# Weight-transpose evacuation in groups of four tiles, and the output store on SyncE's queue, in an eight-core recurrence-and-FFN layer

## The reference, cut to what matters

```python
# u: (4, 4096, 1024) f32; N = 256, HIDDEN = 3072
lam = sigmoid(einsum('btd,nd->btn', u, Wl) + bl)
Bu  = einsum('btd,nd->btn', u, Wb)
h_t = lam_t * h_(t-1) + Bu_t                      # scan over t, h_0 = 0
y   = einsum('btn,dn->btd', H, Wc) + u * Dp
x   = layernorm(u + y)                            # no scale, no bias, eps 1e-5
g   = einsum('bsd,hd->bsh', x, w_gate / 127)      # int32 weights
up  = einsum('bsd,hd->bsh', x, w_up / 127)
out = layernorm(x + einsum('bsh,dh->bsd', silu(g) * up, w_down / 127))
```

## Time and profile before

| | us |
|---|---|
| runs shown: lowest, highest, median of the two | 1896.27, 2077.3, 1986.78 |
| profiled execution, its own time | 1897.56 |
| span of its slowest core (core 7) | 1896.0 |
| spans of the eight cores | 1881.5 to 1896.0 |
| PE busy | 1450.9 (77%) |
| DVE busy | 394.2 (21%) |
| ACT busy | 414.2 (22%) |
| setup of the small weights, up to the first load of u | 0 to 54.3 |
| first matmul of the FFN (line 667) | 772.2 |
| end of the last matmul of the FFN (line 705), about | 1856.6 |

### The profile page before, as it was taken

One profiled execution on the slowest core, in us unless ns is written; L12 is line 12 of the kernel. 1 busy time (PEld: TensorE's weight loads), 2 busy tenths in 40 slices (PEclk: granted clock), 3 DMA queues, 4 the chain that ended last, 5 costly groups with the idle time before them and its releaser, 6 DMA issues.

```text
span 1896.0 us, 19628 instructions; the slowest of 8 cores (1881.5 to 1896.0 us)
## 1 busy us (share of the span) xinstructions
PE 1450.9 (77%) x7216; PEld 720.6 (38%) x7216; DVE 394.2 (21%) x628; ACT 414.2 (22%) x575; POOL 91.0 (5%) x177
## 2 busy tenths in 40 slices
PE   2493846738364333799997999997999997999993
PEld 1342433424222323344443444443444443444441
DVE  2330130401054232122102222103122103212103
ACT  2324142421323444211100311101211002111001
POOL 0001000010100000000010000010000011000010
PEclk9795876859598566899998999997999997999996
DMA  2517265280700000222221322221322222222121
GB/s 67 161 57 170 62 167 122 62 174 16 160 6 1 0 1 0 78 78 78 72 73 45 115 75 78 73 73 56 106 78 74 76 71 79 80 78 78 50 73 50
DMA packets 85165, 142.85 MB, mean 75 GB/s; under 512 B 33360, under 2 KB 34384, under 8 KB 85072
## 3 DMA queue, kind: packets, MB, share of 16 engines
q1 hardware_dynamic: 35152, 70.27, 12.5%
q0 software_dynamic: 18048, 52.44, 12.0%
q10 hardware_dynamic: 31872, 18.88, 3.3%
HBM read 133.17 MB, written 27.26 MB: 85 GB/s over the span
## 4 chain that ended last, share of the span: by engine, by line
PE 66%; DMA 11%; DVE 9%; ACT 7%; issue 5%; DVEq 0%; ACTq 0%; POOL 0%; POOLq 0%; SPq 0%
PE pp L667 35%; PE pp L705 14%; DMA wbufd<-wdT_s 4%; PE ppA L449 3%; PE ppB L471 2%; PE ppA L471 2%; PE ppB L449 2%; DVE stat L232 2%; DMA cvgu<-wu 2%; DMA cvgu<-wg 2%; ACT x1tok L253 1%; PE pbf L279 1%; DVE res L718 1%; ACT t2b L564 1%; ACT stgw L306 1%
## 5 line engine op out<-in xcount | busy, mean ns | idle before, releaser
L667 PE MATMUL pp<-x1hi,wbufg 128*128 128x512 bf16 x768 | 294.5, 383 | 5.1 <-DMA wbufg<-wgT_s 5.1
L705 PE MATMUL pp<-hh_hi,wbufd 128*128 128x512 bf16 x768 | 290.8, 379 | 9.2 <-DMA wbufd<-wdT_s 7.7
L667 PE MATMUL pp<-x1lo,wbufg 128*128 128x512 bf16 x768 | 293.9, 383 | 0.0
L667 PE MATMUL pp<-x1hi,wbufu 128*128 128x512 bf16 x768 | 291.1, 379 | 0.0
L667 PE MATMUL pp<-x1lo,wbufu 128*128 128x512 bf16 x768 | 291.1, 379 | 0.0
L705 PE MATMUL pp<-hh_lo,wbufd 128*128 128x512 bf16 x768 | 290.9, 379 | 0.0
L677 DVE TENSOR_TENSOR hhf<-g_sb,pp 128x512 f32<-128x512 f32 x96 | 66.0, 687 | 457.3 <-PE pp L667 457.3
L683 ACT ACTIVATE hh_hi<-hhf 128x512 bf16<-128x512 f32 x96 | 60.5, 630 | 345.2 <-DVE hhf L677 345.2
L279 PE MATMUL pbf<-idbf,cvgu 128*128 128x128 bf16 x384 | 48.1, 308 | 100.8 <-DMA cvgu<-wu 45.1
L705 PEld LDWEIGHTS pp<-hh_hi,wbufd 128*128 128x128 bf16 x768 | 74.8, 97 | 123.4 <-issue 42.7
L667 PEld LDWEIGHTS pp<-x1hi,wbufg 128*128 128x128 bf16 x768 | 75.9, 99 | 97.6 <-issue 9.1
(11 more groups left out here) (103 smaller groups left out, 1441.9 us busy)
## 6 DMA issues: line engine op xcount, KB each, us to landing
wbufg<-wgT_s SPq DMA_DIRECT2D x96, 256.0 KB, 2.7
wbufu<-wuT_s SPq DMA_DIRECT2D x96, 256.0 KB, 2.7
wbufd<-wdT_s POOLq DMA_DIRECT2D x96, 256.0 KB, 3.0
utok<-u_pre SPq DMA_DIRECT2D x16, 512.0 KB, 5.2
utok<-u_main SPq DMA_DIRECT2D x16, 512.0 KB, 4.6
out<-x1tok POOLq DMA_DIRECT2D x16, 512.0 KB, 3.2
cvwd<-wd POOLq DMA_DIRECT2D x8, 768.0 KB, 10.1
cvgu<-wg POOLq DMA_DIRECT2D x24, 256.0 KB, 5.8
```

What stands on the lines that cost most here:

```text
L667: lambda e: e.matmul(o, l, r, start=st_, stop=sp_)))(
L705: lambda e: e.matmul(o, l, r, start=st_, stop=sp_)))(
```

## The change

Two edits. In the setup, the four copies and four subtractions of a bank, 128 columns each, become one copy and one subtraction of 512 columns. The transposes, the two banks and the tokens stay. In the FFN, the store of each output tile is issued by SP and no longer by POOL, at the same place in the program order and with the same semaphores.

```diff
-                for k, (kind, a, dc) in enumerate(grp):
-                    if kind == "wlb":
-                        hi = wlbT_hi[:, (a * DC + dc) * P:(a * DC + dc) * P + P]
-                        lo = wlbT_lo[:, (a * DC + dc) * P:(a * DC + dc) * P + P]
-                        wtok = "wlbT"
-                    else:
-                        ...
-                    pbk = bank(bidx)[:, k * P:(k + 1) * P]
-                    sc.step("scalar", (lambda o, s: (lambda e: e.copy(out=o, in_=s)))(hi, pbk),
-                            reads=[("pb", bidx)], writes=[wtok])
-                    sc.step("vector", (lambda o, s, h: (lambda e: e.tensor_tensor(
-                        out=o, in0=s, in1=h, op=OP.subtract)))(lo, pbk, hi),
-                        reads=[("pb", bidx), wtok], writes=[wtok])
+                kind0, a0, dc0 = grp[0]
+                cb = (a0 * DC + dc0) * P
+                if kind0 == "wlb":
+                    hi, lo, wtok = (wlbT_hi[:, cb:cb + 4 * P],
+                                    wlbT_lo[:, cb:cb + 4 * P], "wlbT")
+                else:
+                    ...
+                pbk = bank(bidx)[:, 0:4 * P]
+                sc.step("scalar", (lambda o, s: (lambda e: e.copy(out=o, in_=s)))(hi, pbk),
+                        reads=[("pb", bidx)], writes=[wtok])
+                sc.step("vector", (lambda o, s, h: (lambda e: e.tensor_tensor(
+                    out=o, in0=s, in1=h, op=OP.subtract)))(lo, pbk, hi),
+                    reads=[("pb", bidx), wtok], writes=[wtok])
 ...
-                sc.step("gpsimd", (lambda d, s: (lambda e: e.dma_start(out=d, in_=s)))(
+                sc.step("sync", (lambda d, s: (lambda e: e.dma_start(out=d, in_=s)))(
                     out_h[gg * P:(gg + 1) * P, :], x1tok[sl][:, :]),
                     reads=[("x1tokbuf", sl)], sem=f"qo{sl}", n=16)
```

More of the change, by code:

```diff
@@ L344, in build_nc @@
                         lazy=(k < len(grp) - 1))
-                for k, (kind, a, dc) in enumerate(grp):
-                    if kind == "wlb":
-                        hi = wlbT_hi[:, (a * DC + dc) * P:(a * DC + dc) * P + P]
-                        lo = wlbT_lo[:, (a * DC + dc) * P:(a * DC + dc) * P + P]
-                        wtok = "wlbT"
-                    else:
-                        hi = wcT_hi[:, (a * DC + dc) * P:(a * DC + dc) * P + P]
-                        lo = wcT_lo[:, (a * DC + dc) * P:(a * DC + dc) * P + P]
-                        wtok = "wcT"
-                    pbk = bank(bidx)[:, k * P:(k + 1) * P]
-                    sc.step("scalar", (lambda o, s: (lambda e: e.copy(out=o, in_=s)))(hi, pbk),
-                            reads=[("pb", bidx)], writes=[wtok])
-                    sc.step("vector", (lambda o, s, h: (lambda e: e.tensor_tensor(
-                        out=o, in0=s, in1=h, op=OP.subtract)))(lo, pbk, hi),
-                        reads=[("pb", bidx), wtok], writes=[wtok])
+                kind0, a0, dc0 = grp[0]
[4 more added lines that the diff above has]
+                else:
+                    hi, lo, wtok = (wcT_hi[:, cb:cb + 4 * P],
+                                    wcT_lo[:, cb:cb + 4 * P], "wcT")
+                pbk = bank(bidx)[:, 0:4 * P]
[4 more added lines that the diff above has]
+                    reads=[("pb", bidx), wtok], writes=[wtok])
         sc.barrier()
```

## The result

The changed kernel takes 1907.6 us in the median of its runs, against 1895.9 for the kernel before. Run against run, the ratio is 1.0057, with a 95% interval from 1.0045 to 1.0069: it is slower by 0.57%, about 11 us, and the interval lies clear of 1. The comparison leaves out executions in which one half of the chip ran at a lower clock; without them, and with the profiled one of 1904.65 us, the median is 1905.9.

The account below looks back on a forecast made before the run. The prediction took PE's waits to bound the kernel, with PE busy for 77% of the span. From 1897.56 us it took 18.2 for the setup and added 28.4 for three boundaries: 1908 us, range 1896 to 1923.

Parts of the forecast that it names:

- the store's bytes ahead of the load: FFN block boundary: the store's 512 KB go ahead of the weight load on the same queue, taking 1.46 us.
- SP's reaction: FFN block boundary: SP needs about 0.25 us after the last `x1tok` before it issues the store.
- the restart: PE's slow matmuls at low clock after each boundary wait: counted 0 extra, up to 1 us per boundary.
- the end of the span: Landing of the last store on SP's queue: 0.5 us later or some tenths earlier, counted 0.
- Edit 1: Setup: wide copies and subtractions shorten the chain from 36.0 to 17.8 us, saving 18.2 (16.9 to 19.1).
- rival D: Setup: PE's bank refill joins the chain, so wide copies gain only 2.4 us; 1924 us, chance 0.08.
- POOL's part at nothing: FFN: freeing POOL of the stores saves nothing; only `wbufd` loads stand behind them, needed after 24 rounds.
- The wait at a boundary: Three FFN boundaries: next-block loads leave behind the last store, PE waits; 9.5 us each, 28.4 in all.
- the span between 3.25 and 5.9: FFN boundary: microseconds from the store's issue to PE's start, best to worst case; 4.4 taken.
- the bound from `utok`: End of the program: `utok`, 512 KB on SP's queue, takes 3.7 us at its quickest, against 3.2 from POOL.
- Rival B: FFN boundaries: the first loads aren't late, the store edit costs nothing; 1879 us, 1% less, chance 0.05.
- Rival C: FFN boundaries: loads behind the store land very late, 21.2 us lost each; 1943 us, 2.4% more, chance 0.05.

Follow-up runs that it names:

- The fillers: The changed kernel plus 24 matmuls of no use behind the last transposes of blocks 0 to 2; ratio 1.0030 to the kernel before.
- the quicker setup: The changed kernel with next-block loads ahead of the stores, plus separate Wl and Wb tokens, four PSUM banks and a token per group; 1864.5 us, ratio 0.9844.

## Why the prediction was right, and where it was not

It held in the sum: 1908 us forecast, 1905.9 to 1907.6 measured, and the two mechanisms are the ones that the experiments show. What failed is how the answer was put. In "Range and chances" I wrote that about 2% is what a measurement of this kernel can tell from no change, and gave 0.88 to "same". But the forecast's own ends, 1903 to 1917, lay wholly above 1897.6, so its direction was slower (the range of 1896 to 1923 reached only 1.6 us below), and the comparison resolves about 0.12% to either side. The statement was a small but certain slowdown, and the chances hid it. The step that failed there is the 2% taken as the resolution. In the sum itself the mechanism was right and the sizes of four terms were not: the store's bytes ahead of the load (1.46 us taken, 0.7 measured), SP's reaction (0.25 taken, 0.07 measured), the restart (counted 0, measured 2.8 us over three boundaries) and the end of the span (counted 0, measured 1.09 us less).

Point by point:

- **Edit 1.** Forecast 18.2 us, measured 18.05 in the mean of the cores. The wide copy takes 586 ns (0.61 taken), the subtraction 692 (0.69), a group 1.55 (1.55). The refill of a bank stays hidden, so rival D falls. One slip in the working: with a copy of 0.70 its own terms give a saving of 17.1, not 16.9; nothing hangs on it.
- **POOL's part at nothing.** Right as far as the traces show: the down parts, whose loads stand behind these stores in POOL's order, are no shorter with the stores gone, 349.6 us against 348.3.
- **The wait at a boundary.** Forecast 9.5 us each, measured 8.9. SP issues the fourth store 0.07 us after the end of `x1tok`, where I had taken 0.25. That 0.25 was a misreading: the last matmul that read the buffer ends at 1330.05, 0.08 us ahead of the issue at 1330.13 in rows 5, and 1329.89 is the start of the next one:

```profile
1329.67 0.38 PE L667 MATMUL pp<-x1lo,wbufg 128*128 128x512 bf16 x1
1329.89 0.38 PE L667 MATMUL pp<-x1hi,wbufu 128*128 128x512 bf16 x1
```

The load is issued 0.49 us after the store, where I had 0.33. From the load's issue to the first matmul it is 3.6 us and not 4.07. The 512 KB ahead cost 0.7 us, half of the 1.46 that I took for bytes going strictly one behind the other. Store and load thus overlap in part. By the Trainium skill, "DMA: Bandwidth & Descriptors", section "Queues, rings and completion order", a later increment waits for the earlier writes of its engine. The trace agrees: at all 24 boundaries the load lands 0.2 to 1.5 us after the store. Whether this rule or the bytes themselves make up the 0.7 us, no run here separates. From the store's issue to PE's start it is 4.07 us, in the lower half of the span between 3.25 and 5.9, where the prediction had read the rule as pointing to the upper half.

- **The restart.** I counted 0 with up to 1 us per boundary; it is 0.93 us per boundary, at the upper end. I had compared one row with one row, seven slow matmuls with seven. The number scatters from 1 to 9 from core to core and boundary to boundary in the kernel before. In the mean it rises from 6.2 to 10.9, and 4.7 x 0.21 = 1.0 us is about what the gate and up parts got longer. The fillers bear this out: with them these parts are 4.3 us shorter over the three blocks.
- **The end.** I counted 0 for the last store. It is 1.09 us quicker on SP's queue in every core: 11.98 us from the last `x1tok` to the end instead of 13.07. The last store is issued 0.5 us earlier (0.07 instead of 0.55 us behind `x1tok`), lands 0.3 us sooner after its issue (2.67 instead of 2.94), and the rest of the program behind the landing is 0.3 us shorter. It was the bound from `utok` that misled. The Trainium skill, "DMA: Bandwidth & Descriptors", section "Issuing engine by pattern", calls SyncE's path generally the faster one; these 1.09 us agree.
- **The sum.** -18.05 + 26.7 + 2.8 - 1.09 make +10.4; the two rows that no term of mine foresaw (-1.5 and +1.3) about cancel, and the mean span rises by 9.9. The wait was 1.7 us too high and the end 1.1, the restart 2.8 too low. These errors offset, so the hit at 1908 is partly luck.
- **Rival B** (the loads not late) fell with SP's timeline. **Rival C** fell with the landing times: PE starts 3.3 to 4.4 us behind the load's issue at the 24 boundaries of the profile, never near 13.

## What to carry to other kernels

An in-order issuing engine is a dependency that no token shows: before a DMA moves to another engine's queue, list what stands behind it in that program order and when it was issued until now. Here a store that waits for the end of a stage took the next stage's prefetch hostage, and with the prefetch written ahead of it in program order the same two edits gain 1.0% instead of losing 0.6%. And a forecast of a small, certain effect should say its sign, even when it is below the size that one would bother to ship.

## What was not expected of the hardware

- How long PE stays at its lower clock after the same gap differs from core to core of one execution: 1 to 9 slow matmuls behind the three boundaries in the kernel before, 7 to 14 with both edits, and 5 to 14 at the start of block 0. A single row says little about this cost; it takes the mean over cores.
- f32 transposes of 128x128 run at two rates. In the changed kernel's setup the first eight take 1.94 us. In the quicker setup the first two groups of eight take 1.94 and 1.91 us, and from 14.9 on eight take 1.04 to 1.06. The profile's granted clock reads 1.00 in all these stretches, so in this first stretch of the program it doesn't tell them apart.
- SP's issues of 256 KB loads in direct succession stand 0.48 to 0.50 us apart; behind one that took 0.66 us the next came 0.81 us after it.
